# Softplus of the two halves of dt in one instruction each over two neighbouring PSUM banks, and an earlier seed for the second expert layer

## What is computed

```
dt = softplus(dbl[..., :DT_RANK] @ W_dt + b_dt)
h  = exp(dt[:, :, None] * A) * h + (dt * x)[:, :, None] * B[:, None, :]
y  = sum_n h[n] * C[n];   y = (y + xr * D) * silu(z);   out = y @ W_out
```

## Time and profile before

| what | value |
|---|---|
| median of 3 runs | 5945.68 us (5944.47 to 5948.22) |
| profiled execution | 5922.77 us, its span 5920.9 us |
| DVE busy | 5270.1 us (89%) |
| POOL busy | 5155.7 us (87%) |
| PE busy | 4658.8 us (79%), granted clock 0.83 |
| ACT busy | 4531.7 us (77%) |

### The profile page before, as it was taken

One profiled execution on the slowest core, in us unless ns is written; L12 is line 12 of the kernel. 1 busy time (PEld: TensorE's weight loads), 2 busy tenths in 40 slices (PEclk: granted clock), 3 DMA queues, 4 the chain that ended last, 5 costly groups with the idle time before them and its releaser, 6 DMA issues.

```text
span 5920.9 us, 68105 instructions
## 1 busy us (share of the span) xinstructions
PE 4658.8 (79%) x13515; PEld 1447.1 (24%) x13515; DVE 5270.1 (89%) x4473; ACT 4531.7 (77%) x6854; POOL 5155.7 (87%) x2127
## 2 busy tenths in 40 slices
PE   7767788777887788877887778877887778877787
PEld 7222222222222222222222222222222222222222
DVE  1239999999999999999999999999999999999998
ACT  0448888787878877887788888788778887888877
POOL 0029998999999999999999999999999998999998
PEclk9888788878888878887888888888888878887888
DMA  3036767776676767666676767767676766776766
GB/s 96 22 91 165 175 163 175 169 170 169 169 178 164 178 159 176 171 168 167 165 178 166 179 160 176 170 166 174 163 178 168 177 162 172 173 170 168 175 172 153
DMA packets 426039, 960.63 MB, mean 162 GB/s; under 512 B 57824, under 2 KB 58073, under 8 KB 392680
## 3 DMA queue, kind: packets, MB, share of 16 engines
q1 hardware_dynamic: 425704, 957.11, 66.1%
HBM read 772.78 MB, written 184.11 MB: 162 GB/s over the span
## 4 chain that ended last, share of the span: by engine, by line
issue 23%; DVE 21%; PE 14%; DMA 12%; ACT 11%; POOL 7%; SPq 3%; DVEq 1%; ACTq 1%; POOLq 0%
DVE X L1208 14%; DMA bc_d<-bc 5%; PE ps L677 4%; DVE X L1192 4%; POOL X L1295 4%; ACT ps L967 3%; POOL X L1285 2%; DMA lo<-lo_d 2%; DMA xp<-in_x 2%; PE ps L711 2%; DMA lo_d<-bc 2%; PE ps L640 2%; DVE hid L1172 2%; PE ps L682 2%; SPq L465 1%
## 5 line engine op out<-in xcount | busy, mean ns | idle before, releaser
L1295 POOL TENSOR_TENSOR X<-X,cR 128x2048 f32<-128x2048 f32 x768 | 3477.9, 4529 | 62.2 <-POOL carry L1293 0.7
L1208 DVE TENSOR_TENSOR_SCAN X<-ps,carry,X 128x512 f32<-128x512 f32 x2688 | 3261.6, 1261 | 130.7 <-ACT ps L967 107.6
L967 ACT ACTIVATE ps<-hi,amat 128x512 f32<-128x512 f32 x2048 | 1373.4, 682 | 647.3 <-DVE X L1208 643.7
L1285 POOL TENSOR_TENSOR X<-lo,bR 128x2048 f32<-128x2048 f32 x258 | 1168.1, 4528 | 27.7 <-DMA lo<-lo_d 27.0
L1192 DVE TENSOR_TENSOR X<-hi,ps 128x2048 f32<-128x2048 f32 x512 | 1158.3, 2262 | 10.4 <-PE ps L711 10.4
L711 PE MATMUL ps<-X,red 128*32 128x512 f32 x6144 | 900.2, 666 | 334.1 <-POOL X L1295 331.0
L677 PE MATMUL ps<-win,w_u 97*128 97x512 f32 (+1 forms) x2080 | 1110.6, 684 | 8.8 <-DMA win<-xn_d 7.8
L967 ACT ACTIVATE ps<-lo,amat 128x512 f32<-128x512 f32 x1026 | 687.0, 677 | 138.9 <-DVE X L1208 92.2
L692 PE MATMUL ps<-xr,wd 128*96 128x512 f32 (+1 forms) x520 | 451.7, 967 | 334.4 <-ACT xr L922 281.3
L640 PE MATMUL ps<-xp,w 96*128 96x512 f32 x864 | 528.7, 746 | 104.2 <-DMA xp<-in_x 102.7
L677 PEld LDWEIGHTS ps<-win,w_u 97*128 97x128 f32 (+1 forms) x2080 | 372.2, 189 | 664.0 <-issue 651.8
(11 more groups left out here) (116 smaller groups left out, 4224.2 us busy)
## 6 DMA issues: line engine op xcount, KB each, us to landing
hi<-hi_d SPq DMA_DIRECT2D x516, 512.0 KB, 8.3
bR<-bc_d SPq DMA_DIRECT2D x516, 256.0 KB, 4.5
lo<-lo_d SPq DMA_DIRECT2D x516, 256.0 KB, 4.5
cR<-bc_d SPq DMA_DIRECT2D x516, 256.0 KB, 6.9
hi_d<-S SPq DMA_DIRECT2D x258, 256.0 KB, 7.9
y_d<-yf SPq DMA_DIRECT2D x128, 256.0 KB, 8.8
yb<-y_d SPq DMA_DIRECT2D x112, 256.0 KB, 8.5
win<-xn_d SPq DMA_DIRECT2D x130, 196.3 KB
```

Source lines behind the costliest of these rows:

```text
L967: A_(p_a[i % RING][:, :], dt, ACT.Exp, scale=amat[:, column(i):column(i) + 1]).then_inc(s_exp, 1)
L1208: V.tensor_tensor_scan(h, a, h, 0.0 if head else carry[:, i:i + 1], ALU.mult, ALU.add).then_inc(s_scan, 1)
L1285: G.tensor_tensor(batch(par, s), lo[:, LOW:2 * LOW, :].unsqueeze(1).to_broadcast([P, 2, 2, CH]), quads(bR, par, s), ALU.mult).then_inc(s_b ...
L1295: G.tensor_tensor(batch(par, s), batch(par, s), quads(cR, par, s), ALU.mult).then_inc(s_hc, 1)
```

## The change

- The three work banks become one PSUM tensor `work` of 128 x 3 x 512, so that a view over banks 1 and 2 (`p_dt`) exists.
- `S` is laid out anew: `S[:, 0]` low dt, `S[:, 1]` high dt, `S[:, 2]` high `dt * x`.
- Abs, Exp and Ln each run once on 128x1024 instead of once on 64x512 and once on 128x512. The Abs waits for both halves' stores of the body before, and for both `D1` and `D0`.
- ACT's order at the start of a body becomes: `exp_dA` 2; Abs and Exp; `exp_dA` 3; Ln; `exp_dA` 4; `copy_bc`; `exp_dA` 5; `exp_dA` 6.
- DVE runs both `make_dt` before scan 4.
- `seed_x` moves from step 0 of the even body to the end of step 23 of the odd body before it.

```diff
-    for uses in (PRO_LAST, PRO_U, PRO_U, PRO_D, D_BANKS):
+    for uses in (PRO_LAST, PRO_U, PRO_U, PRO_D, D_BANKS + [("Y2", 0)]):
...
-            body(img, q, rev, 1, False, last, rev, p0, second, first, Uses(D_BANKS, base))
+            body(img, q, rev, 1, False, last, rev, p0, second, first, Uses(D_BANKS + [("Y2", 0)], base))
...
+        work = ctx.enter_context(nc.psum_tensor("work", [P, WB, CH], f32))
+        ps += [work[:, i, :] for i in range(WB)]
+        p_dt = work[:, 1:3, :]
...
+            LOG = S[:, 0:2, :]
+            def softplus_start(u, b):
+                act.wait_ge(s_shi, b * 32 + 32)
+                act.wait_ge(s_slo, b * 32 + 32)
+                begin(u, "D1")
+                begin(u, "D0")
+                A_(LOG, p_dt, ACT.Abs).then_inc(s_sp, 1)
+            def softplus_exp(b):
+                act.wait_ge(s_sp, b * 3 + 1)
+                A_(LOG, LOG, ACT.Exp, scale=-1.0).then_inc(s_sp, 1)
+            def softplus_log(b):
+                act.wait_ge(s_sp, b * 3 + 2)
+                A_(LOG, LOG, ACT.Ln, bias=1.0).then_inc(s_sp, 1)
...
                     if i == 0:
-                        if not odd:
-                            seed_x(u, pc)
-                        softplus_start(1, u, n + 1)
+                        softplus_start(u, n + 1)
+                        softplus_exp(n + 1)
                     if i == 1:
+                        softplus_log(n + 1)
+                    if i == 2:
                         copy_bc(u, n + 1)
-                        softplus_log(1, n + 1)
-                    if i == 2:
-                        softplus_start(0, u, n + 1)
-                    if i == 3:
-                        softplus_log(0, n + 1)
...
+                    if i == NT - 1 and odd:
+                        seed_x(ahead, pc + 1)
...
                     if i == 4:
                         make_dt(1, u, n + 1)
+                        make_dt(0, u, n + 1)
                     if i == 6:
-                        make_dt(0, u, n + 1)
```

More of the change, by code:

```diff
@@ L299, in moe_mamba @@
         xf = sb("xf", [C, CH])
-        ps = [ctx.enter_context(nc.psum_tensor(f"ps{i}", [P, CH], f32)) for i in range(8)]
+        ps = [ctx.enter_context(nc.psum_tensor(f"ps{i}", [P, CH], f32)) for i in range(5)]
+        work = ctx.enter_context(nc.psum_tensor("work", [P, WB, CH], f32))
+        ps += [work[:, i, :] for i in range(WB)]
         p_a, p_b, p_y, p_w = ps[0:RING], ps[3], ps[4], ps[5:8]
+        p_dt = work[:, 1:3, :]
         s_ld = sem("weights_loaded")
@@ L318, in moe_mamba @@
         s_pf = [sem(f"work_bank{i}_free") for i in range(WB)]
-        s_sp = [sem("softplus_steps_high"), sem("softplus_steps_low")]
+        s_sp = sem("softplus_steps")
         s_dtx = [sem("dtx_high_ready"), sem("dtx_low_ready")]
@@ L446, in store_low @@
                 wait_alone(s_dtx[1], b + 1)
-                sp.dma_start(lo_d[par, 0:DR, :], S[0:DR, 2, :]).then_inc(s_slo, 16)
+                sp.dma_start(lo_d[par, 0:DR, :], S[0:DR, 0, :]).then_inc(s_slo, 16)
                 sp.dma_start(lo_d[par, DR:P, :], bc[0:DR, :]).then_inc(s_slo, 16)
@@ L457, in store_high @@
                 for k in range(2):
-                    sp.dma_start(hi_d[par, P * k:P * k + P, :], S[:, k, :]).then_inc(s_shi, 16)
+                    sp.dma_start(hi_d[par, P * k:P * k + P, :], S[:, 1 + k, :]).then_inc(s_shi, 16)
             def load_b(b, par):
@@ L986, in _ @@
                 ln_rstd(u, j)
-            last_piece, first, second, rest, _ = prologue_uses()
+            last_piece, first, second, rest, following = prologue_uses()
             copy_gates(last_piece)
@@ L993, in _ @@
             act.wait_ge(s_open, 1)
[L994 to L998, removed]
+            softplus_start(rest, 0)
+            softplus_exp(0)
+            copy_bc(rest, 0)
+            softplus_log(0)
             for i in range(LEAD):
                 exp_dA(0, i, 0)
+            seed_x(following, NCH)
             def body(img, q, rev, odd, head, last, before, p0, u, even, ahead):
@@ L1172, in gate_hidden @@
                 free(u, f"G{m}", V.tensor_tensor(hid[:, m, :], begin(u, f"G{m}")[:, :], hid[:, m, :], ALU.mult))
-            LOG = (S[:, 0, :], S[0:DR, 2, :])
+            LOG = (S[:, 1, :], S[0:DR, 0, :])
             ROWS_OF = (P, DR)
             def make_dt(k, u, b):
-                dve.wait_ge(s_sp[k], b * 3 + 3)
+                dve.wait_ge(s_sp, b * 3 + 3)
                 free(u, f"D{k}", V.scalar_tensor_tensor(LOG[k], p_w[u.at[f"D{k}"][0]][0:ROWS_OF[k], :], 0.0, LOG[k],
@@ L1258, in normalise @@
                 G.tensor_tensor(xnp[:, :], xc[:, :], sq[:, :], ALU.mult).then_inc(s_xn, 1)
-            DT, DTX, ROWS_OF = (S[:, 0, :], S[0:DR, 2, :]), (S[:, 1, :], bc[0:DR, :]), (P, DR)
+            DT, DTX, ROWS_OF = (S[:, 1, :], S[0:DR, 0, :]), (S[:, 2, :], bc[0:DR, :]), (P, DR)
             def times_x(k, u, par):
```

## The result

The changed kernel takes 5999.4 us (median of 4 runs, 5996.47 to 6002.53) against 5945.08 us for the kernel before (4 runs): 1.0095 times as long, 95% interval 1.008 to 1.0109. That is +54 us where +49 was forecast. The clock granted to TensorE was 0.83 of full speed in the profile before and 0.82 in the one after.

What follows compares the result with a forecast made beforehand. DVE was taken as the bound, busy 5270 of 5921 us. Terms 43 + 5 + 5 + 0, less some 4 us, gave +49 us on 5945.7: 5994 us; likeliest case 5970 to 6020, full range 5946 to 6060.

Steps and rivals of the forecast that it cites:

- Busy time of the joined instructions: Abs, Exp, Ln on ACT: 1.00, 1.06 and 1.06 us, 0.54 us less ACT work per body.
- The wait at step 5 of even bodies: DVE's 0.28 us wait at the scan of step 5 goes, in up to 64 bodies: 18 us at most.
- The wait for `D0`, reversed odd +43: Reversed odd bodies: scan 3 stalls by `D0`'s lag behind the old Abs, mean 1.59 us in 27 bodies: +43 us.
- So the stall stays: Reversed odd bodies: nothing in the rest waits for PE or POOL, so the whole +43 us remains.
- no change: Rival: stalls are real but every body kind has give, for instance before `exp_dA` 22; 5946 us, chance 0.10.
- Reversed even +5, forward odd +5: Stalls of 27 and 28 us before scan 3, mostly absorbed by later `gate_y` and `gate_hidden` waits: +5 us each.
- Forward even 0: Forward even bodies: `D0` mostly early, 8 us of stall less 0.28 us in some 24 bodies: 0.
- The later `make_dt`: High half's `make_dt` two steps sooner on DVE stays behind `times_c` on POOL as before: 0.
- `copy_bc` later, 0: `copy_bc` ends 4.2 us later in a reversed odd body, but the window's load hides the store's delay: 0.
- `seed_x`, 0: `seed_x` moved into ACT's idle time before `exp_dA` 2: 0, at most 0.5 us in 32 forward even bodies.
- `D0` in time: Rival: PE gets the upper clock, `D0` ends before the old Abs; -18 to -35 us, 5920 us, chance 0.08.
- `copy_bc` exposed: Rival: the store's landing follows the later copy, 49 + 100 us, 6095 us; chance 0.12 in part or whole.

Runs made afterwards that it cites:

- E8: The kernel after with the second matmul of `D0` left out, so `D0` is ready earlier with other values; 5973.37 us, ratio 1.0063.
- E9: The kernel before with the window's load in two transfers and `seed_x` moved to the odd body, softplus in two chains; 5806.78 us, ratio 0.9757.
- E2: The kernel before with only `seed_x` moved to step 23 of the odd body, softplus in two chains; 5938.49 us, ratio 0.9987.
- E7: The kernel before with the second matmul of `D0` left out, the control for E8; 5945.83 us, ratio 1.0006.
- E3: The kernel before with the store of B and C held back on SP until `exp_dA` of tile 6 is done; 5967.96 us, ratio 1.004.
- E5: The kernel before with the window's load in two transfers, rows 0 to 95 and the row of ones; 5846.34 us, ratio 0.9848.

## Why the prediction was right

The forecast was +49 us and "slower", by a stall before scan 3 as long as `D0` lags behind the old Abs. The mechanism is right. That the total came within 5 us is in part luck: the forecast put the whole loss on the lag, and E8 leaves it only about half. Its steps in order:

- *Busy time of the joined instructions*: within 0.02 us each. ACT is not the bound, and the 49 us of busy time it saved did not return as time. The wait at step 5 of even bodies went, as said (20.7 us before, none after), but a wait before scan 3 took its place. E9, where both are all but gone, is the fastest.
- *The wait for `D0`, reversed odd +43*: 47.5 us of idle, +54.7 us in the sum of these bodies or +38.6 if they are cut on DVE. The right mechanism, shown by E8 (8.3 us left once `D0` is early). The rest of the +54.7 is 6.5 us more before scan 22 of the reversed even body ahead, for `exp_dA` 22 behind its tables. "So the stall stays" was too strong. New waits for PE before L1198 came (22.6 us), and the wait for `exp_dA` 22 in reversed odd bodies went from 38.4 to 3.6 us. That is what the rival "no change" named as its cause; it took back a part of the stall and not the whole.
- *Reversed even +5, forward odd +5*: -7.9 and +1.6 (+11.2 and -6.1 cut on DVE). The stall is in both (39.7 and 24.2 us). In the first `gate_y`'s waits went from 65 to 32 us, against 94 in E2, 91 in E7 and 102 in E8, where there is little or no stall: they took it up, as argued. In the second `gate_hidden`'s went from 50 to 26, but they are 31 in E2 and 28 in E7 already, so how much they took up is not settled.
- *Forward even 0*: +21.4. The later `make_dt` had been called free on POOL, and POOL's wait for it tripled (19 to 64 us from 600 to 5400 us, 19 to 70 over all bodies but the first). But 45 of those 50 us of growth lie in reversed bodies. In forward even ones the wait went from 16.1 to 21.5 us, so it does not explain the +21. There DVE waited 16 us more for `exp_dA` before scans 9, 10 and 14 (26.7, then 43.0). Why those came later is open.
- *`copy_bc` later, 0*: the load behind it starts 10.6 to 11.1 us after the window in all kinds, while the copy came 3.0 to 3.9 us later. E3 shows the cover for 8 us and its end before 9.8; E5 shows its cause.
- *`seed_x`, 0*: -8 us (E2), better than said; I had priced 0.5 us in forward even bodies at most.

How far do sums of single profiles carry? The kernel before, E2 and E7 all lack the joined softplus. Their reversed odd bodies sum to 1362.7, 1363.9 and 1360.1 us, but the forward even ones to 1318.8, 1335.0 and 1352.0, the reversed even ones to 1437.6, 1461.0 and 1467.1 and the forward odd ones to 1332.5, 1311.4 and 1308.7. Only the reversed odd difference stands clear of that spread, by either cut. The three others, the +21.4 among them, do not, so which of the small terms was sized wrongly is not settled; what is firm is that the lag does not make up the whole 54 us.

The Trainium skill, "DMA: Bandwidth & Descriptors", section "Why a DMA increments its semaphore by 16 and not by 1", says that the outermost dimension decides over how many engines a transfer spreads. The runs agree: 96 rows and 1 instead of 97 took the store's landing from 6.8 to 1.6 us.

Of the rivals, "`D0` in time" did not come: over `D0`'s matmuls in reversed odd bodies the granted clock was 0.65 before and 0.62 after. E8 built its condition in another way, and that did not give the 5920 us of that forecast but 27 us more than its control. "`copy_bc` exposed" fell with E3, except for a store later than 8 us. "No change" is out by the time, though its cause was at work in reversed odd bodies, as said above.

## What to carry to other kernels

Joining two instructions joins their waits. Before the 0.5 us of overhead is counted, look when the later input is ready against the start of the earlier instruction, and what stands behind it on the same engine: here 1.6 us of lag outweighed it. Price the give as well: a stall costs nothing where a later wait of the same body hangs on another chain, so sum it by kind of body, on the engine that bounds the kernel, and lay two executions of like kernels beside each other before a sum of 20 us is believed. And a wait of 7 us for a 64 KB store is a question: ask which transfer is ahead of it and over how many rows that one is cut.

## What the runs showed of the hardware

A load of 97 rows of 2 KB ran at 24 GB/s for some 8.5 us. From 2638.8 to 2643.7 us nothing but these rows moved (packets of 2072 bytes), at 23 GB/s, and the 16 DMA engines were busy for 0.06 of the time on average, which is as much as one of the 16. A 64 KB store issued behind it landed after 6.8 us instead of 1.6 (medians, the kernel before and E5), and the residual's load after 9.8 instead of 2.5. Cut into 96 rows and 1 row, the load took that delay with it, and 1.5% of the kernel's time. The page of the kernel before names this load as a releaser for 7.8 us in all; what it cost showed only in the landing times of the transfers behind it.

One ScalarE instruction read two neighbouring PSUM banks: an Abs of 128x1024 took 1.02 us, where 128x512 had taken 0.60 and 64x512 0.57.
